# Attention scales of queries and keys from sums of squares on ScalarE instead of maxima on VectorE

## What is computed

```python
x = x + 0.5 * ffn(layernorm(x))      # ternary weights, top 204 of 2048 hidden values per token
x = x + attention(layernorm(x))
x = x + 0.5 * ffn(layernorm(x))

# attention, 16 heads of 32
ckv = x @ w_kv + b_kv
key = concat(ckv @ w_ku + b_ku, x @ w_kr + b_kr)
q_lat = x @ w_q + b_q
query = concat(q_lat @ w_qu + b_qu, q_lat @ w_qr + b_qr)
value = ckv @ w_vu + b_vu
at = softmax(causal(q @ k.T) / sqrt(32))
out = (at @ v) @ w_o + b_o
```

## Time and profile before

| | |
|---|---|
| time, median of 3 runs | 1183.21 us (1180.74 to 1184.17) |
| the profiled execution: its time, its span | 1186.78 us, 1185.0 us |
| PE busy | 1057.1 us, 89% of the span |
| DVE busy | 869.4 us, 73% |
| ACT busy | 807.5 us, 68% |
| POOL busy | 344.5 us, 29% |
| mean granted clock of TensorE | 0.975 of full speed |

### The profile page before, as it was taken

One profiled execution on the slowest core, in us unless ns is written; L12 is line 12 of the kernel. 1 busy time (PEld: TensorE's weight loads), 2 busy tenths in 40 slices (PEclk: granted clock), 3 DMA queues, 4 the chain that ended last, 5 costly groups with the idle time before them and its releaser, 6 DMA issues. The chain is left out here.

```text
span 1185.0 us, 17838 instructions
## 1 busy us (share of the span) xinstructions
PE 1057.1 (89%) x5862; PEld 475.3 (40%) x5862; DVE 869.4 (73%) x2207; ACT 807.5 (68%) x1196; POOL 344.5 (29%) x385
## 2 busy tenths in 40 slices
PE   0787999998899799999999699999999799998896
PEld 0333455544454233232344233232344345554443
DVE  4778899988984887884335787884324889998893
ACT  5588898898635465567514456667646988989872
POOL 1222344443552041101210041102211135444355
PEclk9989999999999899999999889999999899999999
DMA  9554535534000153210001053210043552664200
GB/s 367 154 108 90 95 59 107 108 74 92 2 1 25 34 111 68 51 38 1 1 23 34 23 104 74 55 38 2 1 80 76 94 98 64 125 125 83 61 19 37
DMA packets 33196, 83.01 MB, mean 70 GB/s; under 512 B 5558, under 2 KB 7993, under 8 KB 29114
## 3 DMA queue, kind: packets, MB, share of 16 engines
q0 software_dynamic: 12544, 47.71, 21.8%
q1 hardware_dynamic: 20538, 33.99, 9.1%
HBM read 64.76 MB, written 4.21 MB: 58 GB/s over the span
## 5 line engine op out<-in xcount | busy, mean ns | idle before, releaser
L879 ACT ACTIVATE arena<-arena,X 128x2048 int8<-128x2048 f32 x154 | 307.9, 2005 | 7.6 <-DVE X L1364 7.1
L939 ACT ACTIVATE arena<-zP,asc 128x512 f32<-128x512 f32 (+3 forms) x384 | 201.1, 583 | 111.8 <-PE zP L720 81.0
L563 PE MATMUL zP<-T,arena 128*128 128x512 f16 x1024 | 246.3, 391 | 0.0
L611 PE MATMUL oP<-T,arena 128*128 128x512 f16 x832 | 198.9, 383 | 2.7 <-DVE arena L1479 2.7
L563 PEld LDWEIGHTS zP<-T,arena 128*128 128x128 f16 x1024 | 102.6, 101 | 124.5 <-issue 14.6
L835 ACT ACTIVATE arena<-zP,sc 128x512 f32<-128x512 f32 x128 | 87.5, 688 | 70.5 <-PE zP L563 70.3
L611 PEld LDWEIGHTS oP<-T,arena 128*128 128x128 f16 x832 | 81.2, 98 | 81.5 <-issue 6.6
L716 PE MATMUL zP<-arena 98*128 98x512 f16 (+3 forms) x384 | 111.1, 335 | 0.9 <-ACT arena L939 0.7
L1593 DVE CUSTOM_DVE_ANT_0 scored<-hP,causal 128x128 bf16<-128x128 f32 (+3 forms) x170 | 80.9, 484 | 23.6 <-PE hP L695 22.7
L695 PE MATMUL hP<-arena 96*128 96x512 f16 (+3 forms) x256 | 83.9, 347 | 14.7 <-DVE mx L1593 12.0
L1160 POOL TENSOR_TENSOR arena<-arena 128x512 f32<-128x512 f32 x16 | 20.4, 1273 | 257.7 <-DVE arena L1623 235.1
(11 more groups left out here) (206 smaller groups left out, 1748.9 us busy)
## 6 DMA issues: line engine op xcount, KB each, us to landing
arena<-bz_row POOLq DMA_DIRECT2D x26, 1024.0 KB, 8.2
arena<-arena SPq DMA_DIRECT2D x168, 64.0 KB, 2.0
x_sb<-bet_row POOLq DMA_DIRECT2D x8, 1024.0 KB, 13.2
arena<-bz_row POOLq DMA_DIRECT2D x6, 768.0 KB, 6.5
arena<-in_w_synT SPq DMA_DIRECT2D x4, 1024.0 KB, 8.0
arena<-in_w_outT SPq DMA_DIRECT2D x4, 1024.0 KB, 14.9
x_sb<-in_b_o POOLq DMA_DIRECT2D x2, 2048.0 KB, 17.3
out_dram<-x_sb SPq DMA_DIRECT2D x16, 256.0 KB, 2.0
```

Source lines behind the costliest of these rows:

```text
L563: mm = pe.matmul(zP[:, c * CW:(c + 1) * CW], part[:, g % 2, k, :], T1[:, k, c * CW:(c + 1) * CW], start=(n == 0 and k == 0), stop=(n == 1 ...
L611: mm = pe.matmul(o, part[:, k, :], T2[:, k, :], start=(c == 0 and n == 0 and k == 0), stop=False)
L879: act.activation(junk[:, counted[0] % 2, :], Z[:, g % ZR, :], ACT.Sign, bias=X[:, 2, k:k + 1], accum_out=S[:, k:k + 1]).then_inc(sm["cnt"], 1)
L939: act.activation(PT[:, m // 4 % 2, h, q0:512], colP[m % 3][:, q0:512], ACT.Exp, scale=asc[:, g, 10:11]).then_inc(sm["exp_done"], 1)
```

## The change

ScalarE passes each of the 16 half planes of a batch twice: first a `Square` with the bias added, whose result goes to memory that split will overwrite (in `parts`) and whose sum over the 512 tokens goes to `mxq` (semaphore `p_sq`), and then the evacuation as before. VectorE's reductions of half planes are gone; of `peak` the small reduction of a group's four sums remains. POOL takes the maximum over the partitions of these sums and, behind it, its square root, as a power of one half. The scale then rests on the root of a sum of squares, which is no smaller than the largest magnitude. `peak` and `scale` are steps of their own in the lists: `scale 2` now stands behind the first two rows of the last key tile, and `scale 3` behind one more row and item 20. `split_hi` waits for the last evacuation of its group, which `q_scale` no longer implies.

```diff
--- before.py
+++ after.py
@@ -56,17 +56,17 @@
     def take(n):
         return [next(r) for _ in range(n)]
 
-    order = [("hi", 1), ("item", 14)] + take(4) + [("peak", 14), ("item", 15), ("lo", 2)] + take(2) + [("lo", 3)] + take(2)
-    order += [("item", 16), ("peak", 15)] + take(2) + [("item", 17), ("item", 18)] + take(2) + [("peak", 16), ("peak", 17)]
-    order += [("item", 19)] + take(2) + [("hi", 2)] + take(2)
+    order = [("hi", 1), ("item", 14)] + take(4) + [("item", 15), ("lo", 2)] + take(2) + [("lo", 3)] + take(2)
+    order += [("item", 16)] + take(2) + [("item", 17), ("item", 18)] + take(2) + [("peak", 17), ("item", 19)]
+    order += take(2) + [("scale", 2), ("hi", 2)] + take(2)
     return order
 
 
 def behind_opening(rows, turn):
 
     r = iter(rows)
-    order = [("peak", 18), ("peak", 19), ("item", 20), ("item", 21), ("hi", 3)]
-    for n in range(3):
+    order = [("peak", 19), ("item", 20), next(r), ("scale", 3), ("item", 21), ("hi", 3), ("item", 22)]
+    for n in range(1, 3):
         order += [next(r), ("item", 22 + n)]
     order += [turn, ("item", 25)]
     for n in range(4):
@@ -898,6 +898,7 @@
 
             def split_hi(b, g):
                 act.wait_ge(sm["q_scale"], b * GROUPS + g + 1)
+                act.wait_ge(sm["p_out"], b * len(ITEMS) + COMPLETE[g] + 1)
                 for w in range(2):
                     act.activation(parts[:, g, w, 0, :], qk[:, w, g, :], ACT.Copy,
                                    scale=asc[:, g, 8 + w:9 + w]).then_inc(sm["split_hi"], 1)
@@ -912,6 +913,9 @@
                 tok = slice(tc * 512, (tc + 1) * 512)
                 col = j if kind == "in" else 4 + j
                 w, g = plane(ITEMS[n])[:2] if plane(ITEMS[n]) else (0, 0)
+                if plane(ITEMS[n]):
+                    act.activation(parts[:, g, w, 0, tok].bitcast(BF16), o, ACT.Square, bias=bcols[:, col:col + 1],
+                                   accum_out=mxq[:, g, w, tc:tc + 1]).then_inc(sm["p_sq"], 1)
                 dst = qk[:, w, g, tok] if plane(ITEMS[n]) else lat[:, j, tok]
                 act.activation(dst, o, ACT.Identity, bias=bcols[:, col:col + 1]).then_inc(sm["p_out"], 1)
 
@@ -1130,9 +1134,9 @@
             def all_max(b, g):
 
                 pool.wait_ge(sm["p_max"], b * GROUPS + g + 1)
-                pool.partition_all_reduce(asc[:, g, 2:4], asc[:, g, 0:2], P, bass.bass_isa.ReduceOp.max)\
+                link(pool.partition_all_reduce(asc[:, g, 2:4], asc[:, g, 0:2], P, bass.bass_isa.ReduceOp.max))
+                pool.tensor_tensor(asc[:, g, 2:4], asc[:, g, 2:4], half[:, :].broadcast_to([P, 2]), ALU.pow)\
                     .then_inc(sm["q_max"], 1)
-                pool.wait_ge(sm["q_max"], b * GROUPS + g + 1)
 
             def core(b):
                 for g in (1, 2):
@@ -1536,21 +1540,17 @@
 
             def project(b):
                 for n in range(IN_CORE):
-                    if plane(ITEMS[n]):
+                    if n in COMPLETE:
                         peak(b, n)
+                        scale(b, plane(ITEMS[n])[1])
                     if ITEMS[n] == ("in", 2, 0):
                         for m in range(2):
                             split_lo(b, m)
 
             def peak(b, n):
-                w, g, tc = plane(ITEMS[n])
-                dve.wait_ge(sm["p_out"], b * len(ITEMS) + n + 1)
-                step(dve.tensor_reduce(mxq[:, g, w, tc:tc + 1], qk[:, w, g, tc * 512:(tc + 1) * 512],
-                                       AX.X, ALU.max, apply_absolute_value=True))
-                if n in COMPLETE:
-                    after(0)
-                    dve.tensor_reduce(asc[:, g, 0:2], mxq[:, g, :, :], AX.X, ALU.max).then_inc(sm["p_max"], 1)
-                    scale(b, g)
+                g = plane(ITEMS[n])[1]
+                dve.wait_ge(sm["p_sq"], 4 * GROUPS * b + sum(1 for e in ITEMS[:n + 1] if plane(e)))
+                dve.tensor_reduce(asc[:, g, 0:2], mxq[:, g, :, :], AX.X, ALU.max).then_inc(sm["p_max"], 1)
 
             def scale(b, g):
 
@@ -1583,6 +1583,8 @@
                         split_lo(b, g)
                     elif kind == "peak":
                         peak(b, g)
+                    elif kind == "scale":
+                        scale(b, g)
                     if kind == "row":
                         h, t, c = e[2:]
                         w = min(512, (t + 1) * P - 512 * c)
```

More of the change, by code:

```diff
@@ L299, in program @@
                  "consts2 r_stats r_rstd bsyn_in hT_sub hT_lo2 ch_dve ch_act ch_pool phase "
-                 "aw_in al_in ab_in a_stats a_rstd a_xn a_turn a_xT p_ps p_out p_max q_max q_scale split_hi split_lo wo_in "
+                 "aw_in al_in ab_in a_stats a_rstd a_xn a_turn a_xT p_ps p_out p_sq p_max q_max q_scale split_hi split_lo wo_in "
                  "stq0 stq1 stq2 stq3 stk0 stk1 stk2 stk3 stack1 stack1k stack2 stack3 sum_out mix_out rec_set unit_set mrow_in row_ps row_max m_set mT_ps m_rows col_ps exp_done mix_done norm_set "
```

## The result

| | before | after |
|---|---|---|
| time, median | 1183.69 us (4 runs, 1180.74 to 1185.44) | 1249.53 us (4 runs, 1247.79 to 1250.93) |
| ratio to before | | 1.056, 95% interval 1.0538 to 1.0583 |
| the profiled execution: its time, its span | 1186.78, 1185.0 us | 1250.93, 1249.1 us |
| mean granted clock of TensorE | 0.975 | 0.953 |

A forecast was written before the change was run, and what follows sets the result against it. It took the latency of the scale relay, decided by POOL's configuration changes, as the bound. Shifts of 31.2 us in batch 0 and 28.6 in batch 1, together 59.8, on the median 1183.21 gave 1243.0 us, range 1226 to 1275.

The forecast's parts named there:

- the signs named for it: In the profile: four MODIFY_POOL_CONFIG per batch at power and all-reduce, POOL idle about 7 us, VectorE some 8 us per scale.
- all-reduce to the end of its power, four times: POOL's all-reduce, change to arithmetic and power of two elements: 8.1 us per scale, 32.4 us per batch.
- scale 0 to the next all-reduce: VectorE's operations, split halves, then ScalarE's queued Squares and evacuations: 9.6 us, with POOL's change back hidden.
- scale 1 to the next all-reduce: The earlier gap of 13.3 us, less VectorE's four peaks, plus one Square: 11.6 us, change back hidden.
- scale 2 to the next all-reduce, the change back: Other work, 3.9 us, no longer covers POOL's change back, so the change itself stands there: 6.9 us.
- L: Price of one POOL configuration change between all-reduce and ordinary arithmetic, taken as 6.9 us in both directions.
- a few us of PE at half clock: PE slowed behind longer idle: a few us, allowed for inside the range 1226 to 1275.
- The Squares: ScalarE's added pass, 0.68 us each, 22 us in all; mostly inside POOL's stalls, without them about 1.0 us on the path.
- Dear changes: Rival: POOL's changes cost 11.3 us towards arithmetic and 9.5 back, giving 1283 us; chance 0.09.
- cheap ones: Rival: POOL's changes cost 2 to 5 us each on idle DMA, giving 1198 to 1224 us; chance 0.08.
- the missing reload: Rival, also "no reload": both POOL codes stay loaded; 1184.4 us, no measurable change, chance 0.04, or faster, chance 0.01.
- its faster variant: Without reloads, VectorE's work alone bounds the opening; fewer peaks return 2.2 us per batch, giving 1179 us; chance 0.01.

## Why the prediction was right

It forecast 1243.0 us, with 1226 to 1275 around it, and slower at 0.95. The mechanism was the predicted one, and the signs named for it are in the profile. Two of them it had misstated: four changes per batch leave eight records at each line, not four, and VectorE's idle time ahead of a scale was 0.65 us before; the 0.41 is counted from the all-reduce's start. Its terms against the trace, batch 0:

| term | forecast | measured |
|---|---|---|
| memset to first all-reduce | 13.5 | 13.58 |
| all-reduce to the end of its power, four times | 32.4 | 33.28 |
| of it the change to arithmetic, each | 6.9 | 7.07 to 7.53 |
| of it the power of two elements | 0.7 | 0.73 |
| scale 0 to the next all-reduce | 9.6 | 9.63 |
| scale 1 to the next all-reduce | 11.6 | 13.80 |
| scale 2 to the next all-reduce, the change back | 6.9 | 5.96 |
| sum, memset to the last scale | 74.0 | 76.29 |

- **The right size of L, for a reason that does not hold.** That 6.9 is so near the measured 7.1 is luck. I took 6.9 us as the stretch of line 1160 with all inputs ready. The run with the later transfer shows that the load began at once, at the end of the instruction ahead, and was simply slower under the transfer: 11.3 us in all, of which 6.9 happened to lie behind the reciprocals. Undisturbed it is 7.1 us. The reason for setting the 11.3 aside, the saturated DMA, was the sound part of the argument.
- **The two directions differ.** 7.1 us to arithmetic, mean of eight, but 5.96 and 6.01 back to the all-reduce, where it shows. The code load that the Trainium skill (GPSIMD Engine Reference, section 2.1, Instruction dispatch) gives, 5.95 us, is what the trace has for the way back. For the way to arithmetic it is 1.2 us too short, and the prediction's estimate from it, 1234, misses the measured time by 15.5 us.
- **The mis-sized term** is "From scale 1 to the all-reduce of group 2 ... 11.6": it was 13.80 us, and 13.84 in batch 1. I took it from the gap before, but PE now comes out of a stall. PE's timeline of after, then that of the kernel with the root on VectorE, the same item 14:

```profile
401.22 0.61 PE L695 MATMUL hP<-arena 96*128 96x512 f16 x1 [6.43 <-DVE mx L1595]
401.62 5.54 PE L658 MATMUL zP<-arena 128*128 128x512 f32 x8
```

```profile
385.64 3.60 PE L658 MATMUL zP<-arena 128*128 128x512 f32 x8
```

Behind 6.43 us of idle time the eight matmuls take 5.54 us instead of 3.60; the window 399 to 406 has a granted clock of 0.53, close to the lower of the two levels, 1.2 GHz against 2.4. With the power gone the same gap is 11.95 us. The work behind the item, from the next row's start at 407.00 and 389.07 to the start of the same pair of plane matmuls at 411.90 and 393.98, takes 4.9 us in both. So the 2 us are the clock's, a second price of the stall. The prediction had put "a few us of PE at half clock" into its range and none into its sum.
- **Behind the last scale** the first column followed after 13.06 us before and 13.82 now: 0.8 us that I took as 0. Batch 1 lost 29.7 us against a forecast of 28.6. The forecast that it loses less than batch 0 held, 29.7 against 34.3. Its cause, that the kernel before takes longer there in batch 1, held only in part: from first all-reduce to first column it took 42.8 and 46.5 us, and three kernels with the relay's work unchanged or nearly so (memset in the power's place, the later transfer, the new order alone) took 42.5 and 44.4, 44.1 and 44.1, 42.3 and 44.4. So at most 2 us of it are the kernel's, and the others are this one execution's.
- **The Squares** were priced at 1.0 us per batch without the stalls; beside the maxima they delayed the fourth all-reduce by 3.2 us, and the program by 7.2. In the changed kernel this did not matter, as forecast, since they lie in POOL's stalls: the power alone, without Squares, was no faster (1252.3).
- **What the 6.5 us between 1243.0 and 1249.53 are.** By the profiled spans the change cost 64.1 us, 4.3 more than the sum's 59.8: 3.1 in batch 0 and 1.1 in batch 1; of the 3.1 the terms above give 2.3 and the stretch behind the last scale 0.8. The other 2 us lie between medians and profiled executions, that of before being 3 us above its median.
- **The rivals.** Dear changes fell with the 7.1 us, cheap ones and the missing reload with the eight loads ahead of the powers and the two ahead of all-reduces that nothing covered. What the other six cost is not seen, being at most the gap that covered them. The "no reload" case put the rest of the change between 1179 and 1184, and the kernel with the root on VectorE, 1179.7, lies where its faster variant stood; but not by that variant's account, VectorE's work alone: with the old order the same kernel stood at 1182.2.

## What to carry to other kernels

On POOL count changes of configuration, not instructions: look in the order of instructions for the bare rows and in the trace for MODIFY_POOL_CONFIG, and add some 6 to 7 us for each that nothing covers, and more behind a heavy transfer (11.3 here). A cheap operation on the wrong side of an all-reduce in a relay costs its change over, its change back, and the clock that PE loses while it stands. If the result only feeds a power of two, take the root in the exponent, on the engine that uses it.

## What the runs showed of the hardware beyond that

- The load starts when POOL reaches the configuration and runs with nothing else on POOL: 7.1 us with DMA at 0.34 of its engines, 11.3 with it at 1.02. The kernel with the root on VectorE, whose transfer of b_o stands where it stood before, shows the long load again, 10.8 and 10.3 us at shares of 1.00 and 0.99. It is hidden as far as POOL would have waited anyway, as ahead of six of the eight all-reduces.
- A memset needs no change: it followed an all-reduce 0.05 us behind it, with no configuration record. Nor do DMA issues: before, POOL goes from its last all-reduce through its loads, two memsets and the DMA of b_o, and the next configuration is line 1160's.
- A load is paid anew each time: the eighth power of the execution waited 7.16 us, as the first did 7.10.
